# Expert stage of a two-choice mixture: pairs of 128-row tiles with an expert per half, in place of 256-row tiles

## What is computed

```
gate_logits = xf @ Wg + bg
top_w, top_i = jax.lax.top_k(gate_logits, TOP_K)          # TOP_K = 2
top_w = jax.nn.softmax(top_w, axis=-1)
w_dense = jnp.sum(jax.nn.one_hot(top_i, E) * top_w[..., None], axis=1)
for e in range(E):
    h = jax.nn.gelu(xf @ W1[e] + b1[e], approximate=False)
    out = out + w_dense[:, e:e + 1] * (h @ W2[e] + b2[e])
```

## Time and profile before

| what | value |
|---|---|
| median of 3 runs | 1441.75 us (1439.1 to 1441.77) |
| the profiled execution, its own time | 1440.63 us |
| its span | 1438.8 us |
| mean granted clock of TensorE | 0.92 of full speed |
| busy: PE, PEld, DVE, ACT, POOL | 81%, 69%, 64%, 48%, 53% of the span |

### The profile page before, as it was taken

One profiled execution on the slowest core, in us unless ns is written; L12 is line 12 of the kernel. 1 busy time (PEld: TensorE's weight loads), 2 busy tenths in 40 slices (PEclk: granted clock), 3 DMA queues, 4 the chain that ended last, 5 costly groups with the idle time before them and its releaser, 6 DMA issues. The chain is left out here.

```text
span 1438.8 us, 38566 instructions
## 1 busy us (share of the span) xinstructions
PE 1172.6 (81%) x12060; PEld 986.1 (69%) x12061; DVE 914.5 (64%) x3298; ACT 689.1 (48%) x1315; POOL 759.3 (53%) x822
## 2 busy tenths in 40 slices
PE   4767654988988866788349999999999999999995
PEld 2545534888888855677337777777777777777774
DVE  6777745988888754766635555565555656565552
ACT  5566643888888754544223333333333333333331
POOL 6233233656666530576725555555555555555555
PEclk9888886999999987777669999999999999999998
DMA  6645538776777635898512222222222222222222
GB/s 164 196 148 183 182 115 190 195 185 181 186 183 185 187 108 186 309 296 269 197 55 36 44 44 44 45 44 44 40 45 45 45 45 45 45 45 45 43 45 26
DMA packets 152162, 169.64 MB, mean 118 GB/s; under 512 B 14286, under 2 KB 144078, under 8 KB 151702
## 3 DMA queue, kind: packets, MB, share of 16 engines
q1 hardware_dynamic: 115942, 131.96, 32.3%
q0 software_dynamic: 21920, 29.38, 11.8%
q10 hardware_dynamic: 14240, 7.55, 2.1%
HBM read 108.22 MB, written 65.49 MB: 121 GB/s over the span
## 5 line engine op out<-in xcount | busy, mean ns | idle before, releaser
L1450 PE MATMUL e_ps_h<-e_xt,w1s 128*128 128x256 f16 x2688 | 320.8, 275 | 29.3 <-DVE e_g_lo L1523 24.9
L1499 ACT ACTIVATE e_gf<-e_ps_h,keep_b 128x256 f32<-128x256 f32 x448 | 203.1, 474 | 267.3 <-PE e_ps_h L1450 267.0
L1465 PE MATMUL e_ps_y<-w2s,e_g_hi 128*128 x1792 | 297.7, 273 | 18.8 <-issue 18.8
L1450 PEld LDWEIGHTS e_ps_h<-e_xt,w1s 128*128 x2688 | 245.8, 98 | 95.3 <-issue 55.5
L813 POOL TENSOR_TENSOR b_p<-b_s,b_p 128x392 f16<-128x392 f32 x196 | 182.6, 932 | 118.6 <-DVE b_p L711 114.8
L1465 PE MATMUL e_ps_y<-w2s,e_g_lo 128*128 x896 | 244.3, 273 | 0.0
L1403 POOL DMA_INDIRECT out<-e_y,e_xg x112 | 180.8, 1614 | 78.4 <-POOLq L1400 44.5
L1523 DVE TENSOR_TENSOR e_g_lo<-e_gf,e_g_hi 128x256 f16<-128x256 f32 x448 | 200.8, 448 | 15.5
L1465 PEld LDWEIGHTS e_ps_y<-w2s,e_g_hi 128*128 128x128 f16 x1792 | 174.8, 98 | 49.9 <-issue 28.2
L1521 DVE CAST e_g_hi<-e_gf 128x256 f16<-128x256 f32 x448 | 138.4, 309 | 54.2 <-ACT e_gf L1499 54.2
L768 ACT ACTIVATE b_s<-b_s,b_neg_max 128x196 f32<-128x196 f32 x392 | 158.5, 455 | 21.3 <-DVE b_neg_max L692 21.1
(11 more groups left out here) (134 smaller groups left out, 1808.9 us busy)
## 6 DMA issues: line engine op xcount, KB each, us to landing
b_v<-v_rows SPq DMA_DIRECT2D x196, 99.5 KB
e_xg<-slots SPq DMA_DIRECT2D x56, 273.0 KB, 2.8
b_k<-qk_hi SPq DMA_DIRECT2D x56, 196.0 KB
a_w_in<-in_w SPq DMA_DIRECT2D x16, 512.0 KB, 3.8
c_w_in<-in_w SPq DMA_DIRECT2D x16, 512.0 KB, 5.5
v_rows<-a_v SPq DMA_DIRECT2D x14, 455.0 KB, 6.3
a_x<-in_x SPq DMA_DIRECT2D x14, 448.0 KB, 5.6
qk_hi<-a_o_hi SPq DMA_DIRECT2D x14, 448.0 KB, 4.6
```

The costliest lines, as they stand in the source:

```text
L1450: mm = pe.matmul(ps_h[:, hc % 4, 0:ST], w1s[:, bass.ds(e, 1), w, a:a + 128].rearrange("p a n -> p (a n)"), xt[:, s, :, 2 * p + k, :], star ...
L1465: mm = pe.matmul(ps_y[:, s, h * C:(h + 1) * C], g[:, s, hc, h * 128:(h + 1) * 128], w2s[:, bass.ds(e, 1), w, a:a + C].rearrange("p a n -> ...
L1499: act.activation(gf[:, hc % 4, :], ps_h[:, hc % 4, 0:ST], ACT.Gelu, bias=b1_sb[:, bass.ds(e * HC + hc, 1)], scale=1.0 / WSCALE).then_inc(g ...
```

## The change

Tiles get 128 rows (ST = 128), and a round handles a pair of them: PAIRS = ((12544 + 8 x 127) // 128 + 1) // 2 = 53 rounds. The two halves of a pair may belong to different experts. So `up` runs each chunk once per half, 12 matmuls of 128 columns in place of 6 of 256; `down` takes W2 by the half's expert; ACT applies gelu by halves with a bias each; `take_y`, `send` and the scatters go by halves, each scatter now waiting for the one before it, and the multiplication stands ahead of that wait. All four expert numbers of a PE round are read at its start. ACT's loop is written out over the 53 pairs. The last `down` uses two of the `ps_h` buffers. The spare slot rows and the `out` rows behind the tokens shrink with ST. The tables in `stage_c` grow, since NT is now 106 and MAXT 49 instead of 56 and 25.

```diff
-ST = 256
+ST = 128
 CHOICES = 2 * TOKENS
-NT = (CHOICES + E * (ST - 1)) // ST
-SLOTS = NT * ST
+PAIRS = ((CHOICES + E * (ST - 1)) // ST + 1) // 2
+NT = 2 * PAIRS
 CAP = TOKENS + ST
-SPARE = 8 * ST
+SPARE = (NT - CHOICES // ST) * ST
...
+        ps_ends = [ps_y[:, h, 0:C] for h in range(2)], [ps_h[:, h, 0:C] for h in range(2)]
...
                 def load(j, n):
-                    row = sp.value_load(row_no[0:1, bass.ds(n, 1)], min_val=0, max_val=ROWS - ST)
-                    sp.dma_start(xg[:, j], slots_dram[bass.ds(row, ST), :].rearrange("(h p) c -> p h c", p=128)
-                                 ).then_inc(xg_in[j], 16)
+                    for h in range(2):
+                        row = sp.value_load(row_no[0:1, bass.ds(2 * n + h, 1)], min_val=0, max_val=ROWS - ST)
+                        sp.dma_start(xg[:, j, h], slots_dram[bass.ds(row, ST), :]).then_inc(xg_in[j], 16)
...
-                def send(j, n):
+                def send(j, h, before):
 
                     s = j % 2
                     pool.wait_ge(yf_ok, 1)
                     pool.sem_inc(yf_ok, -1)
-                    if n is not None:
-                        pool.wait_ge(y_done, 32 * n)
-                        pool.sem_inc(xg_free, 1)
-                    for h in range(2):
-                        last = pool.tensor_scalar(y_sb[:, s, h, :], y_f[:, s, h, :], gate[:, j, h:h + 1], None, ALU.mult)
-                    last.then_inc(y_out, 1)
+                    pool.tensor_scalar(y_sb[:, s, h, :], y_f[:, s, h, :], gate[:, j, h:h + 1], None, ALU.mult
+                                       ).then_inc(y_out, 1)
                     pool.wait_ge(y_out, 1)
                     pool.sem_inc(y_out, -1)
+                    if before is not None:
+                        pool.wait_ge(y_done, before)
+                        if h == 0:
+                            pool.sem_inc(xg_free, 1)
                     pool.sem_inc(y_free, 1)
...
+                def both(j, n, begins, weighs):
+                    send(j, 0, None if begins else 32 * n)
+                    if weighs:
+                        weigh((j + 2) % U)
+                    send(j, 1, 32 * n + 16)
...
                     for hc in range(HC):
                         if not first or hc >= 4:
                             pe.wait_ge(gs_ok, hc - 3 + (0 if first else HC))
-                        n = 0
-                        for k in range(KC):
-                            for w, p in ((0, 0), (0, 1), (1, 0)):
-                                a = k * FH + hc * 128
-                                mm = pe.matmul(ps_h[:, hc % 4, 0:ST],
-                                               w1s[:, bass.ds(e, 1), w, a:a + 128].rearrange("p a n -> p (a n)"),
-                                               xt[:, s, :, 2 * p + k, :], start=n == 0, stop=n == 3 * KC - 1)
-                                n += 1
+                        for h in range(2):
+                            n = 0
+                            for k in range(KC):
+                                for w, p in ((0, 0), (0, 1), (1, 0)):
+                                    a = k * FH + hc * 128
+                                    mm = pe.matmul(ps_h[:, hc % 4, h * ST:(h + 1) * ST],
+                                                   w1s[:, bass.ds(e[h], 1), w, a:a + 128].rearrange("p a n -> p (a n)"),
+                                                   xt[:, s, h, 2 * p + k, :], start=n == 0, stop=n == 3 * KC - 1)
+                                    n += 1
                         mm.then_inc(h_ok, 1)
...
-                                mm = pe.matmul(ps_y[:, s, h * C:(h + 1) * C], g[:, s, hc, h * 128:(h + 1) * 128],
-                                               w2s[:, bass.ds(e, 1), w, a:a + C].rearrange("p a n -> p (a n)"),
+                                mm = pe.matmul(ps_ends[last][h], g[:, s, hc, h * 128:(h + 1) * 128],
+                                               w2s[:, bass.ds(e[h], 1), w, a:a + C].rearrange("p a n -> p (a n)"),
                                                start=n == 0, stop=n == 3 * HC - 1)
                                 n += 1
-                    mm.then_inc(y_ok, 1)
...
+                        mm.then_inc(y_ok, 1)
+
+                def experts(n):
+                    return [pe.value_load(tile_expert[0:1, bass.ds(2 * n + h, 1)], min_val=0, max_val=E - 1)
+                            for h in range(2)]
+
+                def round_(j, n):
+                    after, now = experts(n + 1), experts(n)
+                    up(j + 1, after, False)
+                    turn(j + 2)
+                    down(j, now)
...
-                with act.Fori(0, NT // 2) as i:
-                    for j in range(2):
-                        e = act.value_load(tile_expert[0:1, bass.ds(2 * i + j, 1)], min_val=0, max_val=E - 1)
-                        for hc in range(HC):
-                            act.wait_ge(h_ok, j * HC + hc + 1)
-                            act.activation(gf[:, hc % 4, :], ps_h[:, hc % 4, 0:ST], ACT.Gelu,
-                                           bias=b1_sb[:, bass.ds(e * HC + hc, 1)], scale=1.0 / WSCALE).then_inc(g_ok, 1)
-                    act.sem_inc(h_ok, -2 * HC)
+                for n in range(PAIRS):
+                    e = [act.value_load(tile_expert[0:1, 2 * n + h:2 * n + h + 1], min_val=0, max_val=E - 1)
+                         for h in range(2)]
+                    for hc in range(HC):
+                        act.wait_ge(h_ok, n * HC + hc + 1)
+                        for h in range(2):
+                            last = act.activation(gf[:, hc % 4, h * ST:(h + 1) * ST], ps_h[:, hc % 4, h * ST:(h + 1) * ST],
+                                                  ACT.Gelu, bias=b1_sb[:, bass.ds(e[h] * HC + hc, 1)], scale=1.0 / WSCALE)
+                        last.then_inc(g_ok, 1)
...
+                    for h in range(2):
+                        e = expert(n, h)
+                        dve.wait_ge(y_ok, 1)
+                        dve.sem_inc(y_ok, -1)
+                        if not begins:
+                            dve.wait_ge(y_free, 1)
+                            dve.sem_inc(y_free, -1)
+                        dve.scalar_tensor_tensor(y_f[:, s, h, :], ps_ends[last][h], 1.0 / WSCALE,
+                                                 b2_sb[:, bass.ds(e, 1), :].rearrange("p a c -> p (a c)"),
+                                                 ALU.mult, ALU.add).then_inc(yf_ok, 1)
```

More of the change, by code:

```diff
@@ L1456, in up, with down @@
                         pe.sem_inc(gs_ok, -HC)
-                def down(m, e):
+                def down(m, e, last=False):
                     s = m % 2
@@ L1474, in _ @@
                 turn(0)
-                up(0, expert(0), True)
+                up(0, experts(0), True)
                 turn(1)
-                with pe.Fori(0, NT // U - 1) as i:
+                with pe.Fori(0, LOOPS) as i:
                     for j in range(U):
-                        up(j + 1, expert(U * i + j + 1), False)
-                        turn(j + 2)
-                        down(j, expert(U * i + j))
-                for j in range(U):
-                    n = NT - U + j
-                    if j + 1 < U:
-                        up(j + 1, expert(n + 1), False)
+                        round_(j, U * i + j)
@@ L1486, in _ @@
+                for n in range(U * LOOPS, PAIRS):
+                    if n + 2 < PAIRS:
+                        round_(n, n)
+                    elif n + 1 < PAIRS:
+                        after, now = experts(n + 1), experts(n)
+                        up(n + 1, after, False)
+                        down(n, now)
                     else:
                         pe.wait_ge(gs_ok, HC)
-                    if j + 2 < U:
-                        turn(j + 2)
-                    down(j, expert(n))
+                        down(n, experts(n), True)
@@ L1552, in _ @@
                         take_y(j, U * i + j, False)
[L1553 to L1558 removed]
+                for n in range(U * LOOPS, PAIRS):
+                    if n + 1 < PAIRS:
+                        split(1 - n % 2)
+                    if n + 2 < PAIRS:
+                        take_x(n + 2, n + 2)
+                    take_y(n, n, False, n + 1 == PAIRS)
 def col_windows(q):
```

72 lines of the change are left out of this document (29 added, 43 removed).

## The result

The changed kernel takes **1594.66 us** (median of 4 runs, 1587.04 to 1603.41) against 1441.28 us (4 runs) for the kernel before beside it: ratio 1.107, 95% interval 1.099 to 1.115, slower. The forecast was 1577, and the time lies in its range. All ratios in this document are over runs within 1.5% of the fastest of their kernel, which leaves out two of the four runs of run 4. The profiled execution is one of the lower level: 1587.65 us, span 1585.8, 147.0 more than before.

A forecast was written before the change was run, and what follows sets the result against it. The prediction took PE's array to bound the old kernel at 12.22 us a round and PE's queue the new one at 15.6. Steady part +132.4, ends +3.3 and first loads +1.0 on 1440.6 gave 1577 us, range 1512 to 1612.

The forecast's parts named there:

- The bound of a round: In the expert stage, PE's queue sets the round by register instructions, reads, semaphores and branch: 15.6 us against 12.22.
- The step of 0.127: On PE's queue, each register instruction takes 0.127 us, with the one or two matmuls behind it included.
- `up` 8.13: In `up`, 64 register instructions a round instead of 32 take 8.13 us; the matmuls behind them need 5.38.
- The branch and its addresses: On PE, the loop's branch costs 0.09 us a round, and each computed address of a read 0.10.
- Where the array pauses: At the reads that start a PE round, the array idles for about 1.7 us.
- ACT, DVE, POOL: Hidden under 15.6 us a round: DVE 10.3, POOL 11.4, ACT's two gelus at most 0.74 a chunk.
- Sum: Whole kernel: +132.4 us in the steady part, +3.3 at the ends, +1.0 at SP's first loads, +136.7 in all.
- +2.5 and -2.9: After the last turn, slower `up` and reads add 2.5 us, earlier last scatters give about 2.9 back: 0.
- PE's busy share: Sign in a 100 us window of the expert stage: PE's busy share falls well below nine tenths.
- the queue keeps up: Rival: register instructions of `up` take 0.084 us or less, PE stays the bound, 11.9 us a round, 1386 us; chance 0.07.
- Weight loads set `up`: Rival: weight loads, not the queue, pace `up` at 7.4 us, the round at 13.9, 1493 us; chance 0.07.
- The clock falls: Rival: pauses lower PE's granted clock; below 0.71 it decides, at 0.61 +2.6 us a round, 1715 us; chance 0.06.

The follow-up runs named there:

- run 4: The changed kernel with ACT's loop put back (26 turns of two pairs and one pair behind): median 1607.54 us, ratio 1.107.
- run 3: The changed kernel with a register instruction for each of the 96 matmuls of `up` instead of 64, and two more reads a round: 1955.14 us, ratio 1.339.
- runs 1 and 2: 1: changed kernel, second half takes W1 of the first half's expert, 1431.92 us; 2: kernel before, each `up` matmul split in two of 128 columns, 1437.87 us.
- run 6: The changed kernel with PE's expert numbers kept in two registers without bounds, two reads a round instead of four: 1848.16 us, ratio 1.266.
- run 8: The changed kernel with kept, bounded expert numbers and `down`'s high part taking both parts of W2 in one 512-column matmul: 1459.57 us; without bounds 1606.03 us.
- run 10: The changed kernel with PE's loop of four rounds written out over all 53 rounds: 1587.34 us, ratio 1.103.
- run 7: The changed kernel with PE's expert numbers kept in two registers with bounds, two reads a round instead of four: 1525.89 us, ratio 1.060.

## Why the prediction was right

By its own steps:

- **The bound of a round.** It named the queue, not the array, and 15.6 us. Measured: 15.72 us in the usual pattern (three rounds of 15.57 and one of 16.16), 15.75 over the 50. The step of 0.127 was 0.128, with about one in ten at 0.154 or more and most others at 0.124. `up` 8.13: measured 8.2. `down` 4.06: 4.1. A read 0.65: 0.65. Semaphores 0.15 each: 0.15. The right sizes came from looking for stretches of the old queue in which it was not held back, though those were 2 us long. One term is off by its own working: four reads of 0.65 and 2.5 addresses of 0.10 are 2.85, not 2.87, which leaves the sum at 15.6. (And slice 21 of the earlier trace rows is a 4 and not a nine; the nines begin at slice 22, and nothing hangs on it.)
- **The branch and its addresses.** 0.09 a round plus two extra addresses in the first round: 0.56 us predicted for the long round, 0.59 measured.
- **Where the array pauses.** 1.7 us before each `up`: 1.53 in the mean.
- **ACT, DVE, POOL.** All hidden, as said. A half-width gelu takes 0.363 us, so two of them are near the upper end of the 0.37 to 0.74 given for a chunk, and still under PE's 1.03. `take_y` took 0.424 where 0.69 was the ceiling; POOL's busy share fell from 57 to 47 us in 100. ACT's one table load: right, and run 4 shows that it gains nothing here.
- **Sum.** Span +147.0 where +136.7 was forecast. The difference: 7.3 in the steady part (6 from 0.12 a round, mostly 96 steps of 0.001 more, and 1.3 from the first four rounds, 15.95 to 16.2, in which the program is fetched), 0.75 between the first and third turn, 0.1 at SP's first loads, 2.2 behind the last turn. The last term is a step that failed: +2.5 and -2.9 were meant to cancel. The slower queue cost 3.4 up to the last matmul (26.5 us after the turn instead of 23.1) and the half-tile scatters gave 1.3 back (14.1 us after it instead of 15.4), since the first half's scatter of 1.6 us and its landing still stand in front of the last one. The forecast was off by so little in part because these terms are small beside the 132 us of the rounds.
- **The rest of the distance**, 1587.65 to the median 1594.66, comes from the upper level: the median lies between two runs near 1587 and two near 1602. Nothing in the trace of before pointed to it.

The signs named beforehand held, but one: PE's busy share was to fall "well below nine tenths", and it was 88.7 to 90.7 in six windows of 100 us. (The view also names PE's queue as what ended the idle time, where "issue" was expected.) A matmul record lasts 0.22 us while they begin 0.085 apart, so an array that is starved still looks busy; the distance of starts told it, the share did not.

The rivals: "the queue keeps up" needed a step of 0.084 or less, and run 3 shows 0.124 with a single matmul behind it. "Weight loads set `up`" is excluded by runs 1 and 2. "The clock falls" did not happen: the mean granted clock was 0.95 to 0.98 in six windows of 100 us from 900 to 1500, although the array paused in each round. Only in the longer rounds of other runs, with longer pauses, was it lower in such windows: 0.88 in run 3, 0.90 and 0.92 in run 6. Run 3's register instructions were still 0.124 us apart.

## What to carry to other kernels

Count the register instructions of a dynamically addressed matmul stream before making its tiles smaller: at 0.128 us each in the mean they need more than two 128-column matmuls of 0.056 behind every one, or the sequencer sets the pace while the array still looks nine tenths busy. Read an index once, keep it in a register, and state its bounds where it is taken from there, or each use is checked again. Keep PE's loop body under the 1650 recorded instructions that were fetched only once here, and look at the packets of the instruction queue on the page before and after a change.

## What the runs showed that was not expected

- A matmul of 128 columns with a weight load of its own runs 0.056 us after the one before over 96 in a row (runs 1 and 2), although the weight load's record lasts 0.098. A load's duration was no bound on the pace.
- The queue's lead over the array has a limit, 17 matmuls or 2.9 us in the `down` of run 8; time it gains beyond that is lost.
- A backward branch costs 0.21 us or 3.4 to 5.0, by the length of the body, and next to that edge the same program does the one or the other from run to run.
- Written-out code isn't free either: steps of the queue were 0.004 us longer in the mean in run 10, as in the first pass of each loop, and 110 packets were fetched for the instruction queue instead of 38.
- Bounds left out where a kept register is taken up cost a fifth of the time (ratio 1.266 in run 6, 1.060 in run 7), most of it in the checks and some 40 us in the loop body that they made too long to be fetched once.
